# A one-core transformer block: doubled context by transfers, halves from PSUM, a packed ring, masks of one group by TensorE, twelve rows of placement numbers

## The reference, cut

```python
xn1 = ln(x, g1, be1)
x = x + (mha(xn1, xn1, causal=True) @ W1 + b1)          # 16 heads of 32, scores / DH**-0.5
xn2 = ln(x, g2, be2)
x = x + (mha(xn2, encoder_out, causal=False) @ W2 + b2)  # 64 context rows per batch
x = x + relu(ln(x, g3, be3) @ Wf1 + bf1) @ Wf2 + bf2
# second layer: a gate, softmax over the 1024 rows of a batch, a last layer norm
agreement = sum(text_proj * vision_proj, -1)
out = ln(x + sigmoid(gate_pre) * routing * vision_proj) * gamma + beta
```

## Time and profile before

| | us |
|---|---|
| median of 3 runs | 2275.42 |
| lowest, highest | 2271.31, 2277.21 |
| the profiled execution, device time | 2272.72 |
| its span, first to last instruction | 2270.9 |
| mean granted TensorE clock, share of full | 0.984 |

### The profile page before, as it was taken

The page is one execution under the profiler, slowest core; times in us unless marked ns, Lnnn a source line. Parts: engine busy times, 40 slices in busy tenths (PEclk is TensorE's granted clock), DMA queues, the critical chain, the costliest instruction groups (busy, mean ns, idle before and its releaser), DMA issues.

```text
span 2270.9 us, 32174 instructions
## 1 busy us (share of the span) xinstructions
PE 2161.4 (95%) x11590; PEld 1604.5 (71%) x11590; DVE 1395.7 (61%) x3349; ACT 868.7 (38%) x1610; POOL 932.4 (41%) x943
## 2 busy tenths in 40 slices
PE   7999999999999998889999998999999999999996
PEld 5666666666656664467777776888887887888784
DVE  5577766876786676456666677543455636455546
ACT  4156555655565555534333433221221222121213
POOL 1068767777777778643333342101020202111112
PEclk9999999999999997999999999999999999999998
DMA  7655555555564564211122121320112121121101
GB/s 234 78 82 97 93 85 87 106 89 83 91 111 76 82 96 126 71 56 56 56 70 77 63 80 42 121 84 24 61 61 82 53 74 66 65 66 56 42 33 47
DMA packets 106324, 177.34 MB, mean 78 GB/s; under 512 B 18335, under 2 KB 23455, under 8 KB 106161
## 3 DMA queue, kind: packets, MB, share of 16 engines
q1 hardware_dynamic: 106164, 175.29, 33.1%
HBM read 83.67 MB, written 40.13 MB: 55 GB/s over the span
## 4 chain that ended last, share of the span: by engine, by line
PE 81%; DVE 7%; ACT 5%; issue 3%; POOL 2%; DMA 1%; SPq 0%; POOLq 0%; ACTq 0%; DVEq 0%
PE psum L55 19%; PE psum L56 18%; PE psum L57 18%; PE psum L821 6%; PE psum L766 6%; PE psum L809 5%; PE psum L724 1%; DVE psum L1027 1%; ACT sx L1377 1%; PE psum L830 1%; PE psum L743 1%; PE psum L1327 1%; DMA small<-es 1%; PE psum L1319 1%; PE psum L1268 1%
## 5 line engine op out<-in xcount | busy, mean ns | idle before, releaser
L681 POOL TENSOR_TENSOR es<-es,er 128x512 f32<-128x512 f32 (+3 forms) x640 | 588.0, 959 | 258.4 <-PE psum L821 243.6
L922 ACT ACTIVATE er<-psum 128x512 f32<-128x512 f32 (+3 forms) x640 | 278.4, 471 | 285.6 <-DVE psum L1038 176.2
L1027 DVE CUSTOM_DVE_ANT_0 psum<-psum,mask_ts 128x384 f32<-128x384 f32 (+3 forms) x512 | 249.4, 502 | 152.9 <-PE psum L766 150.6
L766 PE MATMUL psum<-ks,qs 96*128 96x512 f32 (+3 forms) x768 | 260.4, 371 | 7.4 <-DVE mx L1027 3.5
L809 PE MATMUL psum<-qs,ks 100*128 100x512 f32 (+3 forms) x768 | 252.0, 365 | 10.6 <-DVE mx L1027 5.1
L1876 ACT ACTIVATE fy<-psum,cols 128x512 f32<-128x512 f32 x128 | 88.2, 689 | 451.9 <-PE psum L57 451.4
L766 PEld LDWEIGHTS psum<-ks,qs 96*128 96x128 f32 x768 | 139.7, 191 | 115.2 <-issue 32.9
L1031 DVE TENSOR_REDUCE mx<-psum 128x1 fp32r<-128x512 f32 x256 | 175.6, 686 | 61.0 <-PE psum L766 60.0
L55 PE MATMUL psum<-fh,hh 128*128 128x512 f32 x512 | 201.0, 393 | 7.1 <-DVE hl L1977 7.1
L55 PE MATMUL psum<-fah,fh 128*128 128x512 f32 x512 | 202.9, 396 | 0.0
L1975 DVE CAST hh<-fy 128x512 fp32r<-128x512 f32 x128 | 61.2, 478 | 228.5 <-ACT fy L1876 228.1
(11 more groups left out here) (260 smaller groups left out, 4588.7 us busy)
## 6 DMA issues: line engine op xcount, KB each, us to landing
qs<-stage SPq DMA_DIRECT2D x96, 256.0 KB, 5.7
ks<-stage SPq DMA_DIRECT2D x96, 256.0 KB, 8.3
rs<-rs_d SPq DMA_DIRECT2D x32, 256.0 KB
sa_d<-rs SPq DMA_DIRECT2D x32, 256.0 KB, 2.1
sx<-sa_d SPq DMA_DIRECT2D x8, 1024.0 KB, 5.7
xt<-in_x SPq DMA_DIRECT2D x32, 256.0 KB, 6.0
x_d<-xt SPq DMA_DIRECT2D x32, 256.0 KB, 2.0
fw<-in_Wf SPq DMA_DIRECT2D x16, 512.0 KB, 5.3
```

What stands on the lines that cost most here:

```text
L681: e.tensor_tensor(es, es, er, ALU.add).then_inc(s_add.sem, 1)
L766: t = e.matmul(bank1(*s)[:, v * wd:v * wd + wd], Q.qs[par][0:96, i, 128 * ti:128 * ti + 128], Q.ks[par][0:96, i, c0:c0 + wd], start=True, ...
L922: e.activation(dst, bank1("sc", g, c2, j, i)[:, off:512], ACT.Exp, scale=SCALE).then_inc(s_freeS.sem, 1)
L1027: t = e.tensor_tensor_reduce(out=ps, in0=ps, in1=mask_ts[:, 512 - wd:512], scale=1.0, scalar=-3e38, op0=ALU.add, op1=ALU.max, accum_out=mx ...
```

## The change

- `LN_LOAD`, `LN_TURN`, `CUT`, `PROJ`, `PROJ_LONG`, `VALUES`, `MAX` get a row per group for the first four groups, four rows for groups 4 to 11 and four for 12 to 15 (`row`), where before four rows served all (with some numbers of their own for groups 0 and 1). The start (`PROJ_0`, `VALUES_0`) and the `CROSS_` tables change too.
- The ring `er` is packed: a tile takes as many of the 4096 columns as it has, not a slot of 512, and waits for the last earlier tile that lay there.
- In group 14 the mask is added by PE: after each score tile on the diagonal a matmul of the identity with `mask_r`, a copy of the mask that ACT makes once ("mkr"). DVE's "low" is gone there, and ACT's "ex" follows PE.
- "2cd" is now eight transfers from DRAM on SP's queue, 128 partitions by 4 runs of 64 numbers each; the eight copies on DVE are gone.
- "2wb" is cut into four steps of four matmuls, one column each.
- In the first chunk of the second stage ACT writes the biased `sx` into a PSUM bank as well, and DVE's "2sl" reads it from there and no bias.

```diff
+def row(g, n=4):
+    return g if g < n else n + g % n if g < 3 * n else g - n
+MASKED_BY_PE = (14,)
...
+                if s[0] == "sc" and s[3] >= 4 * c2 and g not in MASKED_BY_PE:
                     t += [(a + 0.014, ("low", *s[1:])), (a + 0.028, ("ex", *s[1:]))]
...
-CROSS_AT = 16.793
+CROSS_AT = 16.656
...
+        for at, (g, c2, j, i) in Q.slot_of.items():
+            width = 512 - max(0, 128 * (j - 4 * c2))
+            pos = 0 if pos + width > 4096 else pos
+            under = [n for n, (lo, hi) in held.items() if lo < pos + width and pos < hi]
+            Q.freed_by[at] = max(under, default=None)
...
+                    diag = g in MASKED_BY_PE and j >= 4 * c2
                     t = e.matmul(ps[:, off:512], Q.ks[par][0:100, i, 128 * j:128 * j + 128],
-                                 Q.qs[par][0:100, i, 512 * c2 + off:512 * c2 + 512], start=True, stop=True)
+                                 Q.qs[par][0:100, i, 512 * c2 + off:512 * c2 + 512], start=True, stop=not diag)
+                    if diag:
+                        w.wait_ge(s_mkr, 1)
+                        t = e.matmul(ps[:, off:off + 128], identr[:], mask_r(), start=False, stop=True)
...
-                        if at >= 8:
-                            w.wait_ge(s_add, at - 7)
-                            w.wait_ge(s_pv, Q.pv[Q.slot_of[at - 8]] + 1)
+                        if last is not None:
+                            w.wait_ge(s_add, last + 1)
+                            w.wait_ge(s_pv, Q.pv[Q.slot_of[last]] + 1)
...
+            elif s[0] == "2cd":
+                stacked(w)
+                for k in range(KT):
+                    dst = cd[k // 2][:, 512 * (k % 2):512 * (k % 2) + 512].rearrange("p (b j s) -> p b j s", j=2, s=S)
+                    for j in range(2):
+                        e.dma_start(dst[:, :, j, :], A["ctxT"][128 * k:128 * k + 128, :].rearrange("p (b s) -> p b s", s=S)).then_inc(d_cd.sem, 16)
...
+                if c == 0:
+                    free1(w, *s)
+                    e.activation(bank1(*s), R.sx[:, k, :], ACT.Identity, bias=col("bv_s", k), scale=1.0).then_inc(s_ah.sem, 1)
...
+                if c == 0:
+                    w.wait_ge(s_ah, 2 * k + 2)
+                    e.tensor_tensor(R.al[:, k, :], bank1("2sh", c, k), R.ah[:, k, :].bitcast(F32), ALU.subtract).then_inc(s_al.sem, 1)
```

More of the change, by code:

```diff
@@ L438, in program @@
         O1 = [s for _, s in O1]
[L439 removed]
+        Q.useA, Q.useP, Q.useM, Q.useS, Q.outS, Q.slot, Q.pv, Q.low = {}, {}, {}, {}, {}, {}, {}, {}
         for s in O1:
@@ L452, in program @@
                 Q.slot[s[1:]] = len(Q.slot)
+            if s[0] == "low":
+                Q.low[s[1:]] = len(Q.low)
             if s[0] == "pv":
@@ L456, in program @@
         Q.slot_of = {at: k for k, at in Q.slot.items()}
+        Q.piece, Q.freed_by, held, pos = {}, {}, {}, 0
+        for at, (g, c2, j, i) in Q.slot_of.items():
[3 more added lines that the diff above has]
+            Q.freed_by[at] = max(under, default=None)
+            for n in under:
+                lo, hi = held.pop(n)
+                if hi > pos + width:
+                    held[n] = pos + width, hi
+            Q.piece[at] = slice(pos, pos + width)
+            pos += width
+            held[at] = Q.piece[at].start, pos
         d_rows, d_ct0, d_wv0, d_wt0, d_wg0, d_out0 = (sem(n) for n in ("d_rows", "d_ct0", "d_wv0", "d_wt0", "d_wg0", "d_out0"))
@@ L903, in act1 @@
                     off, n = max(0, 128 * (j - 4 * c2)), 2 * g + c2
-                    if j >= 4 * c2:
-                        w.wait_ge(s_low, 32 * g + 4 * j + i + 1)
+                    if j >= 4 * c2 and g not in MASKED_BY_PE:
+                        w.wait_ge(s_low, Q.low[g, c2, j, i] + 1)
                     else:
@@ L1246, in pe2 @@
             if s[0] == "2wb":
-                freeK(w, 0)
-                w.wait_ge(d_raw2[1], 64)
-                for m in range(4):
-                    for k in range(KT):
-                        t = e.matmul(bank[0][:, m:m + 1], R.raw[1][:, k, 128 * m:128 * m + 128], col("be2", k), start=k == 0, stop=k == 3)
-                t.then_inc(s_fillK.sem, 1)
+                m = s[1]
+                if m == 0:
+                    freeK(w, 0)
+                    w.wait_ge(d_raw2[1], 64)
+                for k in range(KT):
+                    t = e.matmul(bank[0][:, m:m + 1], R.raw[1][:, k, 128 * m:128 * m + 128], col("be2", k), start=k == 0, stop=k == 3)
+                if m == 3:
+                    t.then_inc(s_fillK.sem, 1)
             elif s[0] == "2ck":
```

99 lines of the change are left out of this document (55 added, 44 removed).

## The result

| | median us | lowest, highest | runs | ratio to before, 95% interval |
|---|---|---|---|---|
| before | 2274.92 | 2269.95, 2279.82 | 12 | |
| changed | 2280.76 | 2277.01, 2291.69 | 12 | 1.0031 (1.0021 to 1.0042) |

A forecast was written before the change was run, and what follows sets the result against it. PE, busy 95% of the span, was taken as the bound. 2272.72 - 6.9 - 1.8 + 0.8 - 3.0 - 0.5 = 2261.3 us, and with 1.2 carried for the median 2262.5; range 2251.5 to 2273.

The forecast's parts named there:

- Places by twelve rows: First stage, new batches: earlier maxima cut PE's idle time and the lower clock; gain 3.0 us, from -2 to 6.2.
- its own refutation: At batch starts: the prediction is wrong if PE's idle time per batch start stays at 2.1 us.
- Keys and values: Context keys and values after group 14: short waits, `sx` issued earlier than 947.26; gain 6.9 us, from 0 to 10.
- near 938: Sign in the changed profile: `sx` issued near 938 us, less what earlier batches gave.
- Group 14's term: End of group 14: sum at 901.2 instead of 907.21, 6.0 us earlier, at most 9.8; sign 898 to 903.
- The eight copies, 3.19 us of work: Group 14: DVE's eight "2cd" copies, 3.19 us, stood before the mask that ACT waited for.
- Masks on PE: Group 14: 32 more matmuls, 4.2 us, half of them hidden; cost 0.8 us, from -1.5 to 2.1.
- Packed ring: Outside group 14: ACT's waits for POOL, 9.5 us in 15 places; gain 0.5 us, from 0 to 1.5.
- First chunk: Second stage's start: 0.8 us from the PSUM split, 1.0 from the clock; gain 1.8 us, from 0 to 4.6.
- The small pieces: Rival: doubled context's 256-byte transfers take 20 us or more, values wait 4 us; 2266.5 us, chance 0.07.
- The rival slower: Second "2ck": PE waits for POOL's clears, then weights, and the clock falls; 2282.5 us, chance 0.08.
- The clock: Group 14: no lower clock between 878 and 909 us, or under 10 us; a fall there counts against the prediction.

The follow-up runs named there:

- e1_ld: The changed kernel with one number put back, the load of the last quarter of x for the third batch at 6.440: 2272.42 us, 0.9994.
- e11_rows_new: e3_mech with the first stage's rows of places of the change, the one load put back: 2271.69 us, 0.9992.
- e13_max3: e11_rows_new with the maxima of group 3 at their places of before: 2266.69 us, 0.9962.
- e3_mech: The changed kernel with all tables of places put back to those of before, only the mechanisms kept: 2266.71 us, 0.9971.
- e17_repaired: The changed kernel with the one load of x, the maxima of group 3, CROSS_ONCE and CROSS_KEYS put back: 2262.79 us, 0.9950.
- e15_cross_keys: e3_mech with the change's CROSS_ONCE and CROSS_KEYS: 2274.02 us, 1.0000.
- e16_cross_chunk: e3_mech with the change's CROSS_AT and CROSS_0 alone: 2263.71 us, 0.9948.
- e7_copies_dve: e3_mech with the eight copies of the doubled context back on DVE: 2277.80 us, 1.0022.
- e10_cols_first: e1_ld with DVE's addition into cols at 15.100 instead of 15.142, ahead of the first four kbl steps: 2274.10 us, 0.9999.
- e2_stall: The kernel before with the load of the last quarter of x for the third batch at 6.417 instead of 6.440: 2281.67 us, 1.0031.
- e14_cross_loads: e3_mech with the change's CROSS_LOAD and CROSS_SPLIT: 2267.92 us, 0.9969.

## Why the prediction was wrong

**Places by twelve rows: term 3.0, from -2 to 6.2.** This step failed, by 16 us: a gain of 3.0 was forecast and the rows lose 13. The load cost 8.3 (e1_ld), the maxima of group 3 cost 5.0 (e11_rows_new less e13_max3), and the rest gave 0.0 (e13_max3 less e3_mech; by the ratios 8.4, 6.8 and a gain of 2.0, which comes to 13 as well). The gain rested on DVE's steps at a new batch; PE's busy time in the earlier trace rows was 50.88 and 50.91, and in e17_repaired's same windows it is

```profile
216.00:269.00 53.00, 51.01 (x308) 32.46 (x309) 42.32 (x140) 33.20 (x70) 39.02 (x43) 1.00 0.55 96
...
640.00:693.00 53.00, 51.06 (x310) 33.36 (x310) 42.01 (x136) 33.62 (x69) 40.84 (x46) 1.00 0.54 99
```

so PE's idle time stayed at 2 us, which the prediction had named as its own refutation. The clock's lower level at 642 us is not in that trace, but it is not in e3_mech's either, with the old rows, so it can't be put down to the new ones. The prediction looked at where the maxima end; at the first of the three places, group 3, they start 0.07 of a group later, and that is what took the cover from the statistics. The loss was foreseen in kind ("a table can as well make a new stall") and given 2 us without looking for it. The order of SP's queue showed it: one pair of loads stands ahead of `rs` and `small` where it stood behind them. The prediction looked up the queues that a step is moved past in the transition and not in the table.

**Keys and values: 6.9.** The mechanism of the step, that PE stands briefly at the second "2ck", then 2 to 3 us for the value weights, is in the trace (2.69 and 2.35, forecast under 2 and 2.7). What failed is the sum around it. The term can be read at the issue of `sx`, with the delay of the batches (8.8 us at half 14.0) taken off: 952.48 less 8.8 is 943.7, which is 3.6 us earlier than before and not 6.9. (The prediction's "near 938" does not follow from its own sum, which gives 940.4.) From the sum to that issue it was 45.0 us, where the prediction's numbers give 39.2 and the kernel before took 40.1. In e17_repaired, with the old keys, it was 41.1, and `sx` is issued at 939.02, 8.2 us earlier than before. The prediction took the new places of the keys as part of the gain: they cost 7.3 us (e15_cross_keys less e3_mech), and the old places give the gain without them. Group 14's term was mis-sized the other way. The prediction took 6.0 of at most 9.8 us; the sum, at 907.21 before, came at 907.46, which less 8.8 is 898.7 and 8.5 us earlier, inside the 898 to 903 that the prediction had named. It came at 900.02 in e3_mech and at 897.89 in e17_repaired, 7.2 and 9.3 us earlier.

**The eight copies, 3.19 us of work**. Misread: 1.7 us of work and 1.5 of waiting for POOL. The row merges eight copies and hides that one took 1.78 where the others took 0.28.

**Masks on PE: cost 0.8.** The 32 matmuls cost nothing that shows, and their return stood in other terms; undone, they cost 9.0. **Packed ring: 0.5**, mis-sized, 3.7. **First chunk: 1.8.** Its 0.8 for the split is about right (0.6 to 1.1 in the traces, 0.7 in the medians), with the steps as forecast. The rest was to come from the clock; what came is from the places of the chunk, 3.0 (e16_cross_chunk less e3_mech). **The small pieces** fell: eight transfers of 128 KB were issued from 910.95 on, one after the other, and each landed 2.5 to 2.8 us after its issue. So all 1024 KB were there in some 8 us and not 20; the first "2cv" began at 933.09, and nobody waited for them.

**The rival slower** (2282.5) was near the measured time with the wrong cause: its wait was there, 2.69 us where it asked for over 3, but the transition all in all still gained (9.5 us of delay at half 13.1, 5.3 at the end). The 8.3 us of group 6 made the sign.

**The clock** was at its lower level for 13.7 us in four pieces between 883 and 921, against 27.3 before. The prediction allowed under 10 us between 878 and 909, and there it is 8.6. That it fell in group 14 at all with the masks gone is one of the signs that the prediction had named against itself.

## What to carry to other kernels

Where a table of numbers sets the order, compare the queues and not the numbers: a load that waits, moved ahead of a small transfer on an in-order queue, cost 8 us here, and the order can be seen without a run. Ask of each wait that goes uncovered how much it varies from one execution to the next, not only what it took in the profile. Try mechanisms on the old order first: here they gained 0.3% alone, and with the order made along with them the kernel lost as much.

## What the hardware showed

- A copy on DVE between two SBUF tiles stood 15.8 us while POOL's instructions followed each other, instead of 0.28; in two other traces it stood 1.8 and 3.0 us, until POOL paused, and in a fourth no copy took over 1.09. DVE's maxima and splits, which read PSUM, took 0.6 to 0.7 us in e7_copies_dve beside the same POOL, and the same copies on ACT 0.41.
- The same 256 KB load, issued at the same time in the same order, landed 3.9 us after its issue in one execution and 5.8 in another.
- The executions of one kernel lie along the granted clock: e10_cols_first from 2263.8 us at 0.988 to 2284.6 at 0.978, with the others within some 3 us of that line.
- An idle time of PE of 2.7 us ahead of 20.5 us at the lower clock went with 8.4 us in all (half 2.1 of e11_rows_new against e1_ld). Orders with this place spread by 10.0 to 20.8 us in 12 runs (e1_ld, e11_rows_new, e10_cols_first), orders without it by 5.7 to 16.3 (e2_stall, e14_cross_loads), so the spread has other sources too.
